# A half burst of weighted values and the turning of the next head's maxima, moved between two scores of one pair

## The reference

```python
scores = einsum('bsqhd,bthd->bqhst', qh, kh) * scale   # 4 query groups, 8 key heads, 8 channels a head
probs  = softmax(scores)
a_dot  = einsum('bqhst,bthd->bsqhd', probs, vh)
```

## Time and profile before

| | |
|---|---|
| time of the kernel, median of 3 runs | 735.35 us (734.99 to 736.04) |
| time of the profiled execution | 736.27 us |
| its span, first to last instruction | 734.4 us |
| PE busy over the span | 97% |
| DVE, ACT busy | 79%, 67% |
| first and last turning of maxima | 135.0 and 441.6 us |

### The profile page before, as it was taken

How to read it: one execution, slowest core, us unless ns; L and a number is a source line. 1 busy time by engine, 2 the same in 40 slices (tenths; PEclk the granted TensorE clock), 3 DMA queues, 4 the chain that set the end, 5 groups by cost and what they waited for, 6 DMA issues and landing times.

```text
span 734.4 us, 16311 instructions
## 1 busy us (share of the span) xinstructions
PE 711.4 (97%) x5018; PEld 390.0 (53%) x5019; DVE 577.1 (79%) x784; ACT 491.1 (67%) x886; POOL 137.8 (19%) x298
## 2 busy tenths in 40 slices
PE   8999999899999999999999999899999999999998
PEld 3456544622222222222222223688888888888887
DVE  6276488899999999999999982577777878766755
ACT  2472600289999999999999897656566665656332
POOL 1000000666642222111222220100000000005750
PEclk9999999999999999999999999999999999999999
DMA  9829100167521111011111361051111111122431
GB/s 307 283 73 339 51 0 1 34 194 256 181 66 33 33 34 34 30 25 29 33 33 33 117 227 58 16 172 43 57 50 50 50 50 57 43 101 80 136 109 43
DMA packets 50002, 65.41 MB, mean 89 GB/s; under 512 B 8216, under 2 KB 42928, under 8 KB 49968
## 3 DMA queue, kind: packets, MB, share of 16 engines
q1 hardware_dynamic: 37232, 39.92, 17.1%
q10 hardware_dynamic: 9664, 16.66, 6.9%
q0 software_dynamic: 3072, 8.39, 3.6%
HBM read 40.15 MB, written 24.38 MB: 88 GB/s over the span
## 4 chain that ended last, share of the span: by engine, by line
PE 85%; ACT 7%; issue 3%; DVE 3%; POOL 1%; ACTq 1%; DVEq 0%; POOLq 0%
PE ps L1401 16%; PE ps L1432 14%; PE ps L1456 11%; PE ps L1502 9%; PE ps L1279 7%; PE ps L1536 6%; ACT att L752 5%; PE ps L1304 5%; PE ps L1271 3%; PE ps L1551 3%; PE ps L1493 2%; PE ps L1237 2%; ACT o_sb L711 1%; PE ps L1386 1%; PE ps L1414 1%
## 5 line engine op out<-in xcount | busy, mean ns | idle before, releaser
L1025 DVE TENSOR_REDUCE smax<-ps 128x2 f32<-128x1024 f32 x256 | 296.3, 1215 | 20.8 <-PE ps L1304 19.6
L752 ACT ACTIVATE att<-ps 128x512 f32<-128x512 f32 x512 | 274.2, 596 | 32.8 <-PE ps L1456 23.4
L1401 PE MATMUL ps<-att,v_head 128*32 128x256 f32 x2048 | 164.0, 392 | 6.5 <-ACT o_sb L711 6.1
L1456 PE MATMUL ps<-att 51*128 51x512 bf16 x512 | 158.4, 384 | 3.0 <-ACT att L752 1.7
L1304 PE MATMUL ps<-att 48*128 48x512 bf16 x512 | 155.4, 385 | 1.4 <-DVE smax L1025 1.4
L1432 PE MATMUL ps<-att_r 128*128 128x512 f32 x456 | 118.7, 409 | 2.8 <-DVE att_r L1086 2.8
L1082 DVE TENSOR_TENSOR att_r<-big,att_r 128x1024 fp32r<-128x1024 f32 x76 | 89.7, 1221 | 24.2 <-ACT att_r L732 24.2
L1432 PEld LDWEIGHTS ps<-att_r 128*128 128x128 f32 x456 | 86.2, 190 | 21.4 <-DVE att_r L1086 3.3
L1456 PEld LDWEIGHTS ps<-att 51*128 51x128 bf16 x512 | 35.5, 93 | 110.6 <-DVE smax L1025 40.0
L1401 PEld LDWEIGHTS ps<-att,v_head 128*32 128x32 f32 x2048 | 40.5, 108 | 98.2 <-issue 52.5
L732 ACT ACTIVATE att_r<-big 128x1024 fp32r x74 | 74.3, 1052 | 19.0 <-issue 19.0
(11 more groups left out here) (167 smaller groups left out, 702.9 us busy)
## 6 DMA issues: line engine op xcount, KB each, us to landing
big<-w ACTq DMA_DIRECT2D x8, 1024.0 KB
q_stacks<-big SPq DMA_DIRECT2D x12, 512.0 KB
att<-q_stacks SPq DMA_DIRECT2D x64, 96.0 KB
slot_x<-zeros SPq DMA_DIRECT2D x1, 4992.0 KB, 17.1
e_x<-slot_x SPq DMA_DIRECT2D x39, 128.0 KB, 2.0
slot_y<-xn SPq DMA_DIRECT2D x39, 128.0 KB, 1.7
big<-w ACTq DMA_DIRECT2D x8, 512.0 KB
att<-k_stacks SPq DMA_DIRECT2D x64, 48.0 KB
```

What stands on the lines that cost most here:

```text
L752: act.activation(probs[:, t % 2, g, :], ps[:, RING[turn_of(u) % 3], :], ACT.Exp, scale=SCALE)\
L1025: dve.reduce_max(smax[:, s % 2, :].rearrange("p (half v) -> p half v", half=2)[:, :, v], ps[:, bank:bank + 2, :], X_AXIS).then_inc(max_don ...
L1401: last = pe.matmul(ps[32 * g:32 * (g + 1), 6, queries], v_head[:, s % 2, t, :], probs[:, t % 2, g, queries], start=s % 2 == 0 and t == 0 a ...
L1456: pe.matmul(ps[:, RING[turn % 3], :], k_st[s][rows, P * t:P * (t + 1)], q_st[s][rows, g, :], start=True, stop=True).then_inc(scores_ready, 1)
```

## The change

The turn of the turned maxima goes from 6 to 7, so it falls between scores 6 and 7. The first half burst of the second quarter and the turning of the maxima, which stood after score 5, are issued after score 6. The second half burst stays after score 7. ACT's negation follows exponential 6 in place of exponential 5. Nothing is added or left out.

```diff
-        TURNS, MAX_AT, OUT_AT = 18, 6, 13
+        TURNS, MAX_AT, OUT_AT = 18, 7, 13
...
                                 ins = max_scores((s + 2) % 4, v, 1 - half, 2 * (v % 2))
                                 if half == 1:
                                     ins.then_inc(a_ready, 1)
+                            if v == MAX_AT // 2 and half == 0:
+
+                                weighted_values(i, s, 0, 0, pair)
+                                if not last:
+                                    transpose_max(i + 1, s + 1)
                         if t == OUT_AT // G - 1 and g == PAIR - 1 and s % 2 == 0 and not first:
                             transpose_o(pair - 1, (s // 2 + 1) % 2)
                         if t > 0:
-                            weighted_values(i, s, t - 1, g, pair)
+                            if v != MAX_AT // 2 - 1:
+                                weighted_values(i, s, t - 1, g, pair)
                         elif not first:
                             weighted_values(i - 1, s + 3, ST - 1, g)
-                        if v == MAX_AT // 2 - 1 and not last:
-                            transpose_max(i + 1, s + 1)
```

## The result

The changed kernel takes **747.22 us** (median, 744.84 to 747.68) against 735.69 in the same comparison, a ratio of 1.0152 with a 95% interval of 1.0134 to 1.0170. A second comparison, on another chip, gave 747.50 against 734.04, a ratio of 1.0173 (1.0154 to 1.0193). The forecast was 746.1.

What follows compares the result with a forecast made beforehand. PE was taken to set the pace, with DVE behind. Losses of 8.2 us (odd steps 3 to 27), 1.0 (steps 1 and 29) and 1.5 (even steps 6 to 26) made 10.7, giving 746.1, range 741.0 to 749.0.

Steps and rivals of the forecast that it cites:

- Score 6's wait for reduction 1: Second quarter: moved ahead, score 6 must wait for DVE's reduction 1, ending 0.44 (step 16) or 0.53 (step 17) too late.
- What is queued behind it: Half burst and turning, 0.74 of work, follow waiting score 6; score 7 loses 0.15 in step 16, 0.63 in step 17.
- The price of the wait: Score 6 starts 0.15 after reduction 1 ends; odd steps 3 to 27 lose 0.63, even steps 6 to 26 0.12 to 0.15.
- Step 0: First attention step: no loss was counted, for want of the same pattern.
- No catching up of DVE: DVE's lag at reduction 1 of odd steps stays; the rival that it catches up, about 741.5, had chance 0.08.
- the chain that renews the lag: Reductions 6, 7, 0, 1 run back to back from an even step's reduction 6 to the odd step's wait.
- The saved wait for the output copy: Even steps' half-burst wait, 0.41 each, goes but gives nothing back; the rival that it saves 6.1 us had chance 0.03.
- Negation and its copies: After the turning, 0.92 later in step 17, about 3.5 us left for landing: no cost; rival of late copies, chance 0.03.
- The signs: Traces: odd steps 10.04 us, even 10.23, PE idle at score 6 released by DVE, copy waits down to one or two.

Runs made afterwards that it cites:

- e1: Kernel before with only the turning of the maxima moved between scores 6 and 7, the half burst left after score 5: 736.91 us against 735.56, ratio 1.0017.
- e4: Kernel before with DVE's reductions over only the first 256 of 512 keys: 732.47 us against 735.18, ratio 0.9954.
- e5: Changed kernel with DVE's reductions over only the first 256 of 512 keys: 732.68 us against 735.18 for the kernel before, ratio 0.9963.
- e6: Changed kernel with DVE's reciprocals of even steps moved from ahead of reduction 7 to ahead of reduction 6: 742.25 us against 735.18 for the kernel before.
- e2: Kernel before with only the half burst moved between scores 6 and 7, the turning left after score 5: 751.77 us against 735.56, ratio 1.0224.
- e10: Changed kernel run again unaltered: 747.50 us against 734.04 for the kernel before.
- e9: Changed kernel with ten extra matmuls into an idle bank, ahead of and in step 0: 745.09 us against 734.04 for the kernel before, ratio 1.0146.
- e8: Kernel before with the reciprocals ahead of reduction 6 and extra matmuls ahead of and in step 0: 737.59 us against 734.04, ratio 1.0046.

## Why the prediction was right, and where it was off

- **Score 6's wait for reduction 1: shown.** It starts 0.05 after the reduction's end in both steps above; covered by the burst (e1) the loss is nearly gone; with a DVE that does not lag (e4, e5) it is gone altogether; with a reduction that ends 0.20 earlier (e6) score 6 starts 0.20 earlier.
- **What is queued behind it: shown.** The half burst stands behind the waiting score, and score 7 behind both. In e2 the burst alone, moved behind a waiting score, makes a loss of this kind, though there score 6 waits for exponential 4 at least in even steps. The Trainium skill, "TensorE: Matmul & The Clock Gate", section "What happens when you issue a matmul", keeps matmuls in program order; the trace agrees, with PE idle 0.45 in step 17 while the burst's exponentials had long ended.
- **The price of the wait: mis-sized.** I took 0.15 from the reduction's end to the waiting score, read at score 2. It was 0.05 at score 6 of steps 16 and 17, as of all steps 4 to 27. So odd steps from 5 to 27 lost 0.55 and not 0.63, even ones 0.04 to 0.07 and not 0.12 to 0.15. Outside them the price was 0.15, and step 3 lost 0.64, just as forecast. Steps 1 to 30 came to 8.9, not 10.7.
- **Step 0: taken as nothing, it cost 1.7.** Of this 0.64 is the same wait as elsewhere, which I had left out for want of the pattern; 1.05 goes with the granted clock, which I had not thought of. With the 0.8 ahead of the attention, in which the two kernels do the same (in e10 the changed kernel reaches score 0 at 143.35, close to the 143.27 of the kernel before), this made up for the term before. So the total fits better than its parts, and that is luck. At the same mean granted clock, 0.998, the changed kernel took 744.84 (mean of three executions) and the kernel before 735.26 and 735.49 (twelve and seven in the two larger comparisons): 9.4 to 9.6 is what the change itself costs, and 8.93 for steps 1 to 30 with 0.64 for step 0 comes to the same. The rest of the measured difference, 11.5 and 13.5 us in the two comparisons, goes with the mean clock, as the counts at e9 show.
- **No catching up of DVE: right.** Reduction 1 of step 17 ends 3.29 after score 0 in both kernels; the chain that renews the lag starts behind the change, and shortening it (e6) moved score 6 by just that much.
- **The saved wait for the output copy: right that it gives nothing.** Beside reduction 1, exponential 5 held score 7 in e5.
- **Negation and its copies: right.** Score 0 of step 18 starts with no idle time ahead of it, 5.56 after score 7 in both kernels.
- **The signs.** The half bursts wait for the output copy once and no longer 15 times, and DVE waits longer ahead of reduction 3 (0.44 against 0.37 in step 16), as forecast. That PE's idle time would name DVE held in even steps alone; in odd ones the profile names ACT.

## What to carry to other kernels

Before work is moved out of the way of something, look at what it covers: a burst that seems to delay a matmul may be what the matmul's own wait is hidden under, and an engine that runs its list in order then queues the burst behind the wait. A wait that ends together with another, as the output copy did with exponential 5, is worth nothing until both are gone; a run with one engine's work shortened shows that in one number. And a forecast that fits in total should still be checked stretch by stretch, since here an over-sized wait, a step left out and an unforeseen clock nearly cancelled.

## What the runs showed of the hardware

**The same hand-over from DVE to PE had two prices.** In the changed kernel's step 3, which stands outside the hardware loop, reduction 1 ends at 178.42 + 1.21 = 179.63 and score 6 starts 0.15 later:

```profile
178.42 1.21 DVE L1025 TENSOR_REDUCE smax<-ps 128x2 f32<-128x1024 f32 x1
...
179.78 0.37 PE L1456 MATMUL ps<-att 51*128 51x512 bf16 x1 [0.52 <-ACT att L752]
```

Inside the loop it is 0.05. In the built order score 6 of step 3 carries two waits, for the reduction and for the exponential; in the loop the latter sits on a register instruction ahead of it, and the score waits for the reduction alone. Score 2 of odd steps, from which I took the price, has both waits inside the loop too, and pays 0.15. The steps outside the loop agree (0.15 in steps 0 to 3, 28 and 29 of the changed kernel), and so do those inside it (0.05 to 0.06 in steps 4 to 27). That the second wait is the cause fits these places and was not tried by itself.

**The clock of PE can make the start of a stage vary by 2.5 us from one execution to the next.** Step 0 of the changed kernel took 12.28 at a granted clock of 0.56 to 0.58 (1.2 GHz in most of it) and 9.81 at 1.00 (2.4 GHz). PE's busy time before does not tell the two apart here: from 142 to 146 us it is 2.79 in e10, where the clock stayed up, and 2.89 in the first profile of the changed kernel, where it fell:

```profile
142.00:146.00 4.00, 2.89 (x22) 1.74 (x20) 3.70 (x10) 1.55 (x4) 4.00 (x4) 1.00 0.05 15
```

The Trainium skill, "TensorE: Matmul & The Clock Gate", section "Part 1: The HAM clock gate", says that the lower level is the resting state and activity lifts it. That e9, with its extra matmuls, had 1.00 throughout step 0 agrees with that; e10 had it without them, so these runs do not show that the extra matmuls were needed. And e8's step 28 shows that filling one place does not settle the others.
